# Rebuilding the front of a one-core ViT tower: 64x64 embedding tiles, compact layer norms, first factorisation moved

## The reference

```python
def reference(x, ...):
    h = _L0_tok_ref(x, L0_tok_weight, L0_tok_bias)             # patches 64 rows x 25 columns, strides 64 and 12
                                                               # -> linear to 64 channels -> exact gelu
    h = h + _L0_attn_ref(_layernorm(h, axis=-1), ...)
    h = h + _L0_ffn_ref(_layernorm(h, axis=-1), ...)           # 6 experts, top 2 of them
    return h

def _L0_attn_ref(x, ...):                                      # 8 heads of 8 channels
    qgr, _ = jnp.linalg.qr(q)
    kgr, _ = jnp.linalg.qr(k)
    attn_grass = jnp.einsum('bhnd,bhmd->bhnm', qgr, kgr) ** 2 * grassman_scale
    dots = jnp.einsum('bhnd,bhmd->bhnm', q, k)
    attn_eucl = dots * scale
    attn_riem = dots ** 2 * riem_scale
    a = jnp.concatenate([attn_eucl, attn_riem, attn_grass], axis=1)
    ...                                                        # batch norm, 24 -> 8 channels, softmax
    out = jnp.einsum('bhnm,bhmd->bhnd', a, v)
    ...
    return out @ w_proj.T + b_proj
```

## Time and profile before

| what | us |
|---|---|
| median of 3 runs (lowest, highest) | 371.51 (371.2, 373.81) |
| the profiled execution | 371.06 |
| its span in the profile | 369.3 |
| PE busy | 305.9 (83%) |
| DVE busy | 261.9 (71%) |
| ACT busy | 178.0 (48%) |
| POOL busy | 71.9 (19%) |

### The profile page before, as it was taken

How to read it: one execution, slowest core, us unless ns; L and a number is a source line. 1 busy time by engine, 2 the same in 40 slices (tenths; PEclk the granted TensorE clock), 3 DMA queues, 4 the chain that set the end, 5 groups by cost and what they waited for, 6 DMA issues and landing times.

```text
span 369.3 us, 10042 instructions
## 1 busy us (share of the span) xinstructions
PE 305.9 (83%) x4198; PEld 212.1 (57%) x4198; DVE 261.9 (71%) x595; ACT 178.0 (48%) x309; POOL 71.9 (19%) x67
## 2 busy tenths in 40 slices
PE   4498977788759777878789999989866998999994
PEld 2287564576537655656668776665655544345431
DVE  0887699878787899899964777896988225747241
ACT  0456577622624353534433554848343337595711
POOL 7756424000003222141121231221200000000000
PEclk9799989899867989689988999999998559999989
DMA  8999600000000000000000000000000000010002
GB/s 208 336 328 326 147 0 1 4 4 0 2 0 5 4 2 2 2 3 3 2 4 2 4 2 4 2 3 2 4 2 0 2 0 0 0 26 4 19 0 45
DMA packets 16700, 13.86 MB, mean 38 GB/s; under 512 B 4112, under 2 KB 16400, under 8 KB 16528
## 3 DMA queue, kind: packets, MB, share of 16 engines
q1 hardware_dynamic: 10128, 7.87, 7.8%
q10 hardware_dynamic: 6528, 5.36, 5.2%
HBM read 12.39 MB, written 0.84 MB: 36 GB/s over the span
## 4 chain that ended last, share of the span: by engine, by line
PE 41%; DVE 33%; issue 10%; ACT 9%; ACTq 3%; DMA 1%; POOL 1%; DVEq 0%
PE banks L1373 5%; PE banks L1259 4%; DVE rstd L602 4%; ACT pixels L338 4%; PE banks L1243 4%; ACTq L216 3%; DVE pixels L806 3%; DVE pixels L815 3%; PE banks L1040 2%; DVE pixels L225 2%; PE banks L1270 2%; PE banks L1365 2%; PE banks L1399 2%; PE banks L1284 2%; PE banks L1389 2%
## 5 line engine op out<-in xcount | busy, mean ns | idle before, releaser
L293 POOL TENSOR_TENSOR qbd<-q,weights 128x448 f32<-128x448 f32 x32 | 31.7, 993 | 118.4 <-PE banks L1243 118.3
L1259 PE MATMUL banks<-pixels,convw 64*64 64x204 f32 x768 | 45.1, 367 | 7.3 <-DVE pixels L819 7.3
L1040 PE MATMUL banks<-pixels,weights 128*64 128x204 f32 x416 | 40.8, 359 | 8.6 <-ACT pixels L338 6.4
L1040 PEld LDWEIGHTS banks<-pixels,weights 128*64 128x64 f32 x416 | 35.7, 146 | 14.7 <-issue 11.2
L444 ACT ACTIVATE probs<-pixels 128x408 f32<-128x408 f32 x32 | 17.3, 541 | 52.4 <-DVE pixels L819 52.3
L225 DVE COPY pixels<-pixels 64x1368 f32<-64x1368 f32 x16 | 33.7, 2107 | 12.5 <-DMA pixels<-in_x_dram 12.1
L1259 PEld LDWEIGHTS banks<-pixels,convw 64*64 64x64 f32 x768 | 29.6, 143 | 15.3 <-issue 9.4
L931 DVE TENSOR_TENSOR pixels<-pixels,banks 128x408 f32<-128x408 f32 x24 | 13.6, 576 | 32.9 <-PE banks L1389 20.0
L1243 PE MATMUL banks<-kbd,qbd 64*64 64x102 f32 x1024 | 32.4, 266 | 2.2 <-issue 1.1
L1284 PE MATMUL banks<-vbd,pixels 115*51 115x18 f32 x512 | 18.8, 207 | 15.5 <-DVE pixels L806 13.3
L1284 PEld LDWEIGHTS banks<-vbd,pixels 115*51 115x51 f32 x512 | 15.6, 133 | 26.2 <-DVE pixels L806 21.6
(11 more groups left out here) (161 smaller groups left out, 536.6 us busy)
## 6 DMA issues: line engine op xcount, KB each, us to landing
pixels<-in_x_dram ACTq DMA_DIRECT2D x24, 218.0 KB, 9.9
pixels<-in_x_dram SPq DMA_DIRECT2D x24, 218.0 KB, 11.1
weights<-in_w_dram SPq DMA_DIRECT2D x1, 1200.0 KB, 14.3
out_dram<-pixels SPq DMA_DIRECT2D x8, 102.0 KB
weights<-in_w_dram SPq DMA_DIRECT2D x1, 432.0 KB, 4.0
```

Of the source, the lines that this page charges most:

```text
L293: pool.tensor_tensor(qbd[u][:, :].rearrange("p (c h i) -> p c h i", c=QB, h=H), qv.unsqueeze(2).to_broadcast([128, QB, H, NI]), w("headmas ...
L1040: last = nc.tensor.matmul(bank[g % 2][64 * half:64 * half + 64, (e % 2) * SN:(e % 2 + 1) * SN], w("tok")[:, v * C:(v + 1) * C], src, start ...
L1259: last = nc.tensor.matmul(bank[2 + r][64 * to:64 * to + 64, 0:4 * N], convw[64 * r:64 * r + 64, k * HI:(k + 1) * HI], src[64 * r:64 * r + ...
```

## The change

What it does, part by part:

- **Loads.** All pixel transfers are issued by SP, with 128 partitions: rows 0 to 127 of an image in one, the third strip of two images in another. Six a step as before, `RAWS` is 3. The weights come in three pieces.
- **Sort.** DVE copies phases 0 to 7 of each step (128x1824), ACT phases 8 to 11 (128x912). POOL sorts nothing. Sorted pixels are kept by group, in two buffers.
- **Embedding.** `embed(g, u0, u1)`: 25 taps x 2 row halves x 2 column halves of a 64x64 tile on 204 columns, over both steps of a group; taps are kept in two row orders (`taps`, two copies at the start). It is written in pieces with other work between them. Both groups' results use banks 0 and 1, so a group waits for the gelu of the one before.
- **Norms.** The variance is four matmuls that give 102x8 numbers, DVE adds eps (`variance_eps`), POOL raises them to -1/2 (`inverse_std`), and `broadcast` spreads them by eight matmuls of 64x102. The same for the second norm. ACT's square root and DVE's reciprocal of 128x408 are gone; ACT does the centered copy in the front.
- **First half ahead.** All of groups 0 and 1 up to the Gram matrices and `first_rows`/`gram_rows_first` comes ahead of embeddings 2 and 3.
- **Second half's Gram matrices.** Instead of `gram_blocks` on DVE, ACT copies them out (`gram_out`), and `gram_rows_second` on PE picks the blocks with 128 small matmuls. `qr_load(1)` comes after step 1 of the loop, and the 17 pieces are spread anew over steps 1 to 9.
- v is made by group (`values_of`), and q and k share banks 4 and 5 with the token transposes.

```diff
@@ loads and sort
+        def to_phases(eng, copy, e, lo, hi, done):
+
+            g, k = divmod(e, 2)
+            eng.wait_ge(S[f"pix{e}"], 16 * 6)
+            eng.wait_ge(S["raw_pads"], 1)
+            if g >= ROWS:
+                eng.wait_ge(S["embed"], g - ROWS + 1)
+            src = raw(e).rearrange("p (s c u) -> p u s c", s=2, u=SW)
+            copy(phases(g)[:, lo:hi, :, k, :], src[:, lo:hi]).then_inc(S[done], 1)
...
-            for e in range(STEPS):
-                to_phases(pool, pool.tensor_copy, e, 1, 1)
...
+            def inverse_std(g, tag=""):
+                pool.wait_ge(S[f"eps{tag}_s"], g + 1)
+                pool.tensor_tensor(norm_parts(rstd, g, tag), norm_parts(var_eps, g, tag), minus_half[0:TT, 0:8],
+                                   ALU.pow).then_inc(S[f"pow{tag}_s"], 1)
+                pool.wait_ge(S[f"pow{tag}_s"], g + 1)
@@ ACT
+            def gram_out(t):
+                act.wait_ge(S["gram_mm"], t + 1)
+                nc.scalar.activation(gram_rows(t), gram_bank(t), ACT.Copy).then_inc(S["gs_done"], 1)
@@ DVE
-            def reciprocal_ln(g, tag="", parts=(0, 1)):
-                if parts[0] == 0:
-                    dve.wait_ge(S[f"std{tag}_done"], g + 1)
-                r = slot(rstd, g)[:, parts[0] * SN:(parts[-1] + 1) * SN]
-                nc.vector.reciprocal(r, r).then_inc(S[f"rcp{tag}_done"], len(parts))
...
+            def variance_eps(g, var_bank, tag=""):
+                dve.wait_ge(S[f"var{tag}_mm"], g + 1)
+                nc.vector.tensor_scalar(norm_parts(var_eps, g, tag), bank[var_bank][0:TT, 500:508], EPS, None,
+                                        ALU.add).then_inc(S[f"eps{tag}_s"], 1)
+
+            def scale_ln(g):
+                dve.wait_ge(S["bc_mm"], g + 1)
+                dve.wait_ge(S["xc_done"], g + 1)
+                nc.vector.tensor_tensor(n_sb[:, gcols(g)], slot(xc, g), bank[3][:, 0:GN], ALU.mult).then_inc(S["xn_done"], 1)
...
-            step(0, 0)
-            qr_load(1)
-            factorise(0)
-            factorise(1)
-            at_step = {1: ((), (2,)), 2: ((3,), (4,)), 3: ((5,), (6,)), 4: ((), (7,)), 5: ((8,), ()), 6: ((9,), (10,)), 7: ((11,), (12,)),
-                       8: ((13,), (14,)), 9: ((15,), (16,))}
-            for s in range(1, 14):
+            at_step = {1: ((), (0, 1)), 2: ((2,), (3,)), 3: ((4,), (5,)), 4: ((6,), (7,)), 5: ((8,), (9,)), 6: ((10,), (11,)),
+                       7: ((12,), (13,)), 8: ((14,), (15,)), 9: ((), (16,))}
+            for s in range(0, 14):
                 mid, after = at_step.get(s, ((), ()))
                 step(s, s % 2, s >= 6, lambda: [factorise(i) for i in mid])
+                if s == 1:
+                    qr_load(1)
@@ PE
+            def embed(g, u0, u1):
+
+                if u0 == 0:
+                    pe.wait_ge(S["sort_v"], 2 * g + 2)
+                    if g >= 1:
+                        pe.wait_ge(S["gelu_done"], 4 * g)
+                    else:
+                        pe.wait_ge(S["taps_done"], 2)
+                for u in range(u0, u1):
+                    if u == DVE_PHASES[2 * g]:
+                        pe.wait_ge(S["sort_a"], 2 * g + 2)
+                    j = u // SW
+                    for r in range(2):
+                        rr = slice(64 * r, 64 * r + 64)
+                        for s in range(2):
+                            src = phases(g)[rr, u % SW, s].rearrange("p k (a j) -> p (k a) j", j=PER)[:, :, j:j + NW]
+                            last = nc.tensor.matmul(bank[r][64 * s:64 * s + 64, 0:2 * EN], tap(u, r), src,
+                                                    start=(u == 0), stop=(u == PW - 1))
...
+            def variance(g, var_bank, tag=""):
+                for t in range(4):
+                    last = nc.tensor.matmul(bank[var_bank][0:TT, 500 + 2 * t:502 + 2 * t], slot(sq, g)[:, t * TT:(t + 1) * TT],
+                                            w("avg")[:, 0:128:64], start=True, stop=True)
+                last.then_inc(S[f"var{tag}_mm"], 1)
+
+            def broadcast(g, bc_bank, tag=""):
+                pe.wait_ge(S[f"pow{tag}_s"], g + 1)
...
+            def gram_rows_second():
+
+                pe.wait_ge(S["gs_done"], BT)
+                for n in range(D):
+                    for hh in range(4):
+                        for i in range(4):
+                            h = 4 * (i % 2) + hh
+                            last = nc.tensor.matmul(bank[7][32 * i:32 * i + 32, n * 32 + hh * D:n * 32 + (hh + 1) * D],
+                                                    grams[:, (n * H + h) * 32:(n * H + h + 1) * 32],
+                                                    ident[:, 32 * i + hh * D:32 * i + (hh + 1) * D], start=True, stop=True)
+                last.then_inc(S["g_mm"], 1)
...
             step(0, 0)
-            qr_operands(1)
-            for s in range(1, 6):
+            step(1, 1)
+            first_rows(1)
+            gram_rows_second()
+            for s in range(2, 6):
                 step(s, s % 2)
```

771 lines of the change are left out of this document (419 added, 352 removed).

## The result

The changed kernel takes 427.91 us (median of 4 runs, 422.1 to 431.63) where the kernel before takes 371.36 beside it: a ratio of 1.141, 95% interval 1.128 to 1.155. The profiled execution took 429.64 us. The forecast was 362.0 with a range of 356 to 369.

What follows compares the result with a forecast made beforehand. No engine is full in the late front, DVE paces steps 0 to 13, and PE is full or nearly so afterwards. 371.06 - 9.7 + 3.3 - 2.3 - 0.5 = 361.9, given as 362.0 us, range 356 to 369.

Steps and rivals of the forecast that it cites:

- loading: Pixel loads and sorting at the start: one queue gives 340 GB/s, so embedding 0 can start at 15.4 us.
- 224 as the worst case at 13%: Rival on pixel loads: one queue gives only 224 GB/s, a step takes 6.0 us, whole kernel 367 us; chance 13%.
- the 9% for "slower": Rival on embedding: four 64x64 tiles don't run abreast, 0.181 us a matmul, 400 take 72 us, whole 394; chance 9%.
- SP needs to issue a step in 4 us ... a small risk: Pixel loads: SP must issue each step in 4 us, with as many rows to describe as both queues had together.
- pixels landing after 45: Sign in the new profile that the forecast is wrong: pixels still landing after 45 us.
- pivots behind the norm of group 2: First factorisation on DVE: group 2's norm waits for PE until 84.0 us, so an 18 us lead shrinks to 5.
- Embedding: Embedding on PE: 100 matmuls a group at 0.101 us, 10.1 us a group, with 9.1 as the lower end.
- POOL's power: Power of eight columns on POOL: between nothing and 1.1 us each, three where PE waits; 1.0 us added.
- To the first dots: Late front, from pivots to main loop: 26.8 us plus 1.5 for clock and 1.0 for POOL; first dots at 113.7, 9.7 earlier.
- DVE's stall: Before the pivots: DVE stands for 12 us waiting for PE, with the pivots, signs and everything behind them queued.
- Steps 0 to 13: Early main loop, paced by DVE: second factorisation's first two pieces end 12.2 us after first dots, was 8.9; 3.3 us given back.
- Second norms: Second norms, without reciprocals and table loads: 2.3 us gained in the first half's, 0.5 in the expert part.

Runs made afterwards that it cites:

- rows-first kernel: Changed kernel with the third strip's transfers cut with rows outermost (64 partitions, two images each) instead of two images outermost: 374.49 us, ratio 1.010 to the kernel before.
- two queues: Changed kernel with third strips cut rows outermost, and the second half's transfers issued by ACT's queue instead of SP's: 378.87 us, ratio 1.025 to the kernel before.
- the wait filled: Changed kernel with third strips cut rows outermost, plus three unread float32 matmuls on PE behind q and k of group 2: 372.44 us, ratio 1.009.
- DVE let through: Changed kernel with third strips cut rows outermost, and DVE's norm instructions of groups 2 and 3 moved behind pivots and signs: 370.61 us, median of 4 runs.
- the variance wide: Changed kernel with third strips cut rows outermost, and each second-norm variance matmul writing 128 columns instead of 2: 371.28 us, ratio 0.999 to the kernel before.
- loads mended, the variance wide and DVE let through: Changed kernel with rows-outermost third strips, 128-column second-norm variance and DVE's norm instructions behind pivots and signs: 365.62 us, ratio 0.987 to the kernel before.

## Why the prediction was wrong

**The step that failed** is loading: "At 340 all steps but the first two land before their sort's turn". The rate was 111 GB/s. I asked of the new transfers how many queues and how many partitions they had, took 340 for the value, and 224 as the worst case at 13%. I had the diff's `x[b0 + a:b0 + a + 3:2, ...]` before me and didn't ask for its outermost dimension; every transfer of the kernel before has its 64 rows there. No rival had a rate below 224, so no chance stood where the time fell (the 9% for "slower" was for another mechanism, at 394). "SP needs to issue a step in 4 us ... a small risk" named the place at which it showed, for a wrong reason: 12.6 us of issues a step, each some 2 us long with the transfer engines a third busy, where the same queue issues a step in 3.7 us when the engines keep up. The rule "pixels landing after 45" told it at once: the last sort is at 107.56.

**With that one step mended the front is the forecast's up to the pivots, but the whole is not.** The rows-first kernel takes 374.49 us, 1.0% over the kernel before, where the forecast had 2.6% under: what it missed besides is at the first dots (6 us) and in the expert part, below. Forecast against the rows-first trace: embedding 0 starts 15.4 / 16.2 and ends 27.7 / 27.3; q of group 0 at 42.8 / 43.7; elimination from 61.8 / 64.4 (its copy of the identity took 1.80 us for 0.28), end 71.2 / 73.8; pivots behind the norm of group 2 at 84.6 / 84.7, the wait on PE 12 / 10.3 us. (The prediction has the pivots at 84.6 in one line and counts on from 84.4 in the next; the 0.2 change nothing.) The loads ran at 264 GB/s in place of 340, and PE was late by 0.9 us at most up to q.

**Embedding** was sized 0.101 us a matmul; at full clock 104 records in 4.72 us are 0.091, the lower bound I gave. The slower rival (0.181) is out. POOL's power took 1.64 us for eight columns, above my upper bound of 1.1, and PE waited 0.21 us for it once in the rows-first front: an operation can be mis-sized and cost next to nothing.

**To the first dots:** 113.7 forecast, 119.8 in the rows-first trace, 113.8 in that with two queues. Most of the 6 us goes with the half clock from 89 to 103 and again from 110 to 116, for which I had 1.5: in the three traces with rows first and full clock from 89 to 104 whose fronts differ from it (two queues, the wait filled, DVE let through) the first dots are at 112.5 to 113.8, and with the same front and 1.00 there at 116.72. That DVE's stall would hold nothing but what DVE has queued was wrong too: for 2 us it held ACT's gelu and with it PE.

**Steps 0 to 13** were to give back 3.3; from first dots to row maximum 14 it is 84.1 against 80.8, so 3.3. The sum is right by luck in its parts: the small matmuls took 5.3 us for 3.9, the two pieces ended 18.7 us after the first dots and not 12.2, since I left out the second dots and half clock (the first row maximum came 6.8 us after the first dots for 4 to 5), and later steps won some back (row maxima 8 to 12 in 19.1 us for 20.5).

**Second norms:** of the first half 1.3 us gained for 2.3. In the expert part I had 0.5 us gained, and it lost 6.3 in the changed kernel and 10.2 in the rows-first one. The term that I left out is the clock: the mean granted there is 0.88 before, 0.80 and 0.76 in these two, and the half clock behind the two-column variance is part of that. The broadcast adds 1.6 us on a full PE at full clock, 2.67 in the changed kernel's trace. With the variance wide the part takes 88.1 to 89.8 us at 0.86 to 0.90, against 88.2: nothing gained, up to 1.6 lost. With loads mended, the variance wide and DVE let through the change is worth 1.3%, not the 2.6% of the forecast: some 9 us earlier at the first dots, 4 given back in the loop, nothing from the norms.

## What to carry to other kernels

Read the outermost dimension of both sides of every transfer that a change rewrites, before its bytes and its queue; a DMA share far under 1 while each issue takes 2 us was the sign here of one that is too small. Where order is written by hand, ask of a stall what stands behind it on each engine in turn. What a run of very narrow matmuls costs may lie behind it, in the granted clock.

## What was unexpected of the hardware

- With two images outermost in four of six transfers a step, the rate fell within each step to 45 GB/s at a DMA share of 0.14 (264 GB/s at 1.12 with rows outermost), and a second queue with the same shapes added nothing (106 against 111 GB/s).
- Behind 16 records of two columns on a full PE, the granted clock was 0.50 (1.2 GHz) for 7 to 10 us in seven traces of eight, and at the other such place for 3 to 7 us in four of eight; written 128 wide, in none of six at either.
- 256 records of 8 columns come with gaps of 1.8 to 2.5 us for which the profile shows no reason; splitting them did not move the gap. What causes them is open.
- POOL raised 102x8 numbers to a power in 1.64 us, has 1.10 for 128x384 of a subtraction.
